# A hybrid attention and mixture-of-experts kernel on one core: 48 down projections in three rounded products, an opening cut into tiles, and the router's weights inside the actor's matrix

## The reference, cut to what matters

```python
probs = softmax(x @ router_w.T)                                # 8 experts
a_h = gelu(x @ actor_w1.T + actor_b1)                          # 50 hidden
sampled_k = argmax(clip(a_h @ actor_w2.T + actor_b2, -30, 30)) + 1
mask = rank(probs) < sampled_k                                 # keep the first k experts
scores = where(mask, probs, 0)
for e in range(8):
    g = x @ gate_w[e].T;  u = x @ up_w[e].T                    # 336 hidden each
    out += scores[:, e] * ((silu(g) * u) @ down_w[e].T)
```

## Time and profile before

| | us |
|---|---|
| median of 3 runs | 513.47 |
| lowest and highest | 507.74 and 513.87 |
| the profiled execution | 508.82 |
| its span, first to last instruction | 507.0 |
| mean granted TensorE clock | 0.997 |

### The profile page before, as it was taken

How to read it: one execution, slowest core, us unless ns; L and a number is a source line. 1 busy time by engine, 2 the same in 40 slices (tenths; PEclk the granted TensorE clock), 3 DMA queues, 4 the chain that set the end, 5 groups by cost and what they waited for, 6 DMA issues and landing times.

```text
span 507.0 us, 6599 instructions
## 1 busy us (share of the span) xinstructions
PE 490.1 (97%) x2152; PEld 350.5 (69%) x2152; DVE 297.5 (59%) x705; ACT 247.6 (49%) x435; POOL 294.6 (58%) x306
## 2 busy tenths in 40 slices
PE   7798899999999999999999999999999999999997
PEld 6576666677676666767677677776767676666666
DVE  3647343746767795497844889459673443723332
ACT  3286637356725674238552387425671345223221
POOL 4344778348759393493564737546455555665554
PEclk9999899999999999999999999999999999999999
DMA  8600000000000000000000000000000000000000
GB/s 241 228 0 2 0 0 2 0 1 1 1 1 1 0 0 2 1 2 0 1 0 2 0 1 1 0 2 21 1 0 1 1 22 0 0 1 21 0 2 21
DMA packets 7933, 7.38 MB, mean 15 GB/s; under 512 B 732, under 2 KB 7772, under 8 KB 7900
## 3 DMA queue, kind: packets, MB, share of 16 engines
q1 hardware_dynamic: 7900, 6.97, 4.5%
HBM read 5.91 MB, written 1.05 MB: 14 GB/s over the span
## 4 chain that ended last, share of the span: by engine, by line
PE 74%; DVE 6%; ACT 3%; issue 2%; POOL 1%; DVEq 0%; ACTq 0%; POOLq 0%
PE bank L1150 23%; PE bank L1000 14%; PE bank L1002 13%; PE bank L1001 13%; PE bank L1201 3%; PE bank L1104 1%; DVE t L929 1%; PE bank L1189 1%; PE bank L1020 1%; POOL t L566 1%; PE bank L1158 1%; ACT sl L678 1%; ACT xn L582 1%; PE bank L1138 1%; PE bank L1112 1%
## 5 line engine op out<-in xcount | busy, mean ns | idle before, releaser
L566 POOL TENSOR_TENSOR t<-t,sl 128x512 f32<-128x512 f32 x105 | 136.2, 1301 | 111.2 <-DVE t L929 86.8
L678 ACT ACTIVATE sl<-bank 128x512 f32<-128x512 f32 x168 | 98.9, 595 | 161.3 <-PE bank L1002 151.6
L1150 PE MATMUL bank<-t,WD 128*128 128x512 f32 x328 | 161.6, 592 | 0.0
L929 DVE TENSOR_TENSOR t<-bank,sbc 128x512 f32<-128x512 f32 x105 | 72.2, 688 | 89.9 <-PE bank L1002 88.8
L1000 PE MATMUL bank<-xhF,WGh 128*128 128x512 f32 x168 | 98.9, 589 | 3.4 <-ACT sl L678 2.7
L566 POOL TENSOR_TENSOR t<-t,sbc 128x512 f32<-128x512 f32 x63 | 81.4, 1318 | 8.9 <-ACT sbc L672 8.0
L1150 PEld LDWEIGHTS bank<-t,WD 128*128 128x128 f32 x328 | 61.7, 188 | 28.6 <-issue 15.1
L929 DVE TENSOR_TENSOR t<-bank,sl 128x512 f32<-128x512 f32 x63 | 42.9, 685 | 55.7 <-ACT sl L678 25.2
L1000 PE MATMUL bank<-xhF,WUh 128*128 128x512 f32 x168 | 67.4, 401 | 1.4 <-DVE t L929 1.4
L1002 PE MATMUL bank<-xhF,WUl 128*128 128x512 f32 x168 | 66.6, 397 | 0.0
L1001 PE MATMUL bank<-xlF,WUh 128*128 128x512 f32 x168 | 66.5, 396 | 0.0
(11 more groups left out here) (184 smaller groups left out, 669.7 us busy)
## 6 DMA issues: line engine op xcount, KB each, us to landing
stage<-in_gate SPq DMA_DIRECT2D x7, 192.0 KB, 5.7
stage<-in_up SPq DMA_DIRECT2D x7, 192.0 KB, 6.0
WD<-in_down SPq DMA_DIRECT2D x7, 192.0 KB, 6.0
X<-in_x SPq DMA_DIRECT2D x4, 256.0 KB, 5.7
out<-X SPq DMA_DIRECT2D x3, 256.0 KB, 2.3
raw<-in_small SPq DMA_DIRECT2D x1, 388.0 KB, 5.3
out<-X SPq DMA_DIRECT2D x2, 128.0 KB, 1.9
raw<-in_small SPq DMA_DIRECT2D x1, 192.0 KB, 2.7
```

The costliest lines, as they stand in the source:

```text
L566: pool.tensor_tensor(t2[k % NT2][:, :], t2[k % NT2][:, :], by[:, :], ALU.mult).then_inc(a_done, 1)
L678: act.activation(sl[k % NSL][:, :], bank[k % 2][:, :], ACT.Silu).then_inc(silu_done, 1)
L929: dve.tensor_tensor(t2[k % NT2][:, :], bank[2 + k % 2][:, :], by[:, :], ALU.mult).then_inc(t2_done, 1)
L1150: pe.matmul(OACC[:, :], WD[:, c, :], t2[k % NT2][:, :], start=(c == 0), stop=(c == CH - 1 or k == TAIL[0] - 1))\
```

## The change

It has three parts.

**Down projections.** For 48 of the 168 chunks, chosen by the planner from slot 29 on and none of TAIL, ACT rounds `t2` into a high part (`ah`, three buffers), DVE writes the low part over `t2` (step "al"), and PE adds three rounded passes in place of one fp32 product. `WD` is split once, in seven pieces, ACT the high and POOL the low part (step "wd", every second slot from slot 26). A chunk is taken when the planner's running loads for DVE, ACT and POOL are below three limits. A fp32 down product of another chunk keeps its form.

**Opening.** The head mask is built in two halves, the first ahead of the norm. The three norms that DVE does signal each tile, and PE begins with the first tile. The sums of squares are computed ahead of the similarity. The residual of batch 0 is added tile by tile from four banks. The transposes of the first F norm go to two banks and are split in halves, and the first two passes of gate 0 start before the low half of the tokens is there.

**Routing.** The router's eight columns sit at rows 64 to 71 of the actor's matrix, so that the actor's three passes give the logits too. ACT copies 72 rows in place of 50, and PE transposes the eight rows for four tiles (a new step "rt", one slot later), and DVE reads the logits from that bank. The exponential and its sum come one slot later in the list. The two bank turns of a routing step are now one for "route" and one for "rt".

Besides, `qF`/`kF` share their space with `ql`/`kl`, and `bt` with `PT`; a bank that "byx" frees counts as free one slot later, and the copies of the next transposed scores wait for it.

```diff
+SPLIT_FROM, WD_FROM = CH + 8, CH + 5
+NAH = 3
-F_STEPS = [(0, "stats"), (2, "xn"), (4, "xT"), (5, "xl"), (6, "route"), (7, "rexp"), (7, "inner", 0),
-           (10, "inner", 1), (9, "rsum"), (12, "rrank"), (12, "tanh"), (13, "gelu"), (15, "act"),
+F_STEPS = [(0, "stats"), (2, "xn"), (4, "xT"), (5, "xl"), (6, "route"), (7, "rt"), (7, "inner", 0), (8, "rexp"),
+           (10, "inner", 1), (10, "rsum"), (12, "rrank"), (12, "tanh"), (13, "gelu"), (15, "act"),
-            awo=(0, 0, .5), am=(.3, .3, 0), am2=(.3, .3, 0), y=(.9, 0, .6), route=(2, 1.1, .3), rexp=(0, 2.7, 0),
+            awo=(0, 0, .5), am=(.3, .3, 0), am2=(.3, .3, 0), y=(.9, 0, .6), route=(.7, 1.1, 0), rt=(.4, 0, .4), rexp=(0, 2.7, 0),
+COST |= dict(ah=(0, .6, 0), al=(0, 0, .9))
+DVE_LOAD = dict(uk=.7, al=.9, stats=1.4, xl=.7, ar=.6, ascale=.5, amax=.6, awo=.5, y=.7, yT=.7, rt=.8, rsum=3.6, rrank=2.9,
+                gelu=1.7, actk=1.6, bv=.7, bsp=1.2, byx=2.4)
+DVE_ROOM, DEBT_ACT, POOL_LEAD = 0.7, 1.0, 1.5
...
+    def halves(k):
+        room = debt[0] < DEBT_ACT and dve_load[0] < DVE_ROOM + DVE_LOAD["uk"] and pool_free[0] < k + POOL_LEAD
+        for j in split:
+            if ("al", j) not in done and slot_of.get(("ah", j), last) < k:
+                add(("al", j))
+                debt[1] += COST["al"][2]
+        j = seen[0]
+        while j < len(um_end) and um_end[j] < k + 0.5 and slot_of["um", j] < k:
+            weights = slot_of.get(("wd", j % CH // WCH), last) + 1 < k
+            if j >= SPLIT_FROM and j not in TAIL and weights and room:
+                split.append(j)
+                add(("ah", j))
+                debt[0] += COST["ah"][1]
+            seen[0] += 1
+            if j in split:
+                break
+            j += 1
...
-            if j < len(um_end) and um_end[j] + AFTER_POOL <= k and (j % CH or j == 0 or block_end[j // CH - 1] + OACC_REST < k):
+            if j in split:
+                due = slot_of.get(("al", j), last) < k
+            else:
+                due = j < seen[0] and um_end[j] + AFTER_POOL <= k
+            if due and (j % CH or j == 0 or block_end[j // CH - 1] + OACC_REST < k):
...
+        halves(k)
         products(k, 2)
+        if wds and k >= WD_FROM and k % 2:
+            add(wds.pop(0))
+            debt[0] += 0.5
...
@@ POOL @@
+            head_mask(range(H // 2))
                     if seq == 0:
-                        head_mask()
+                        head_mask(range(H // 2, H)).then_inc(consts_ready, 1)
+                if kind == "wd":
+                    pool.wait_ge(wdh_ready, s[1] + 1)
+                    pool.tensor_tensor(WDl[:, at, :], WD[:, at, :], WDh[:, at, :].bitcast(F32), ALU.subtract).then_inc(wdl_ready, 1)
@@ ACT @@
+                    if (what, b) == ("F", 0):
+                        act.wait_ge(half_full, 1)
+                        act.activation(xhF[0][:, 0:T // 2], bank[3][:, 0:T // 2], ACT.Copy).then_inc(xh_half, 1)
-                    act.activation(xa[:, :], m_bank(t + 1)[0:AH, :], ACT.Identity, bias=cols[0:AH, 4:5])
+                    act.activation(xa[:, :], m_bank(t)[0:R0 + E, :], ACT.Identity, bias=cols[0:R0 + E, 4:5])
+                if kind == "ah":
+                    k, i = s[1], split_at[s[1]]
+                    act.wait_ge(a_done, k + 1)
+                    if i >= NAH:
+                        act.wait_ge(down_done, split[i - NAH] + 1)
+                    act.activation(ah[i % NAH][:, :], t2[k % NT2][:, :], ACT.Copy).then_inc(ah_done, 1)
@@ DVE @@
+                    if s == ("y", 0):
+                        for i in range(NT):
+                            ...
+                            r = dve.tensor_tensor(X[:, i, :], bank[i][:, 0:P], X[:, i, :], ALU.add)
+                if kind == "al":
+                    k, i = s[1], split_at[s[1]]
+                    dve.wait_ge(ah_done, i + 1)
+                    dve.tensor_tensor(t2r[k % NT2][:, :], t2[k % NT2][:, :], ah[i % NAH][:, :].bitcast(F32),
+                                      ALU.subtract).then_inc(al_done, 1)
@@ PE @@
-                    for i in range(NT):
-                        a, o = slice(i * P, i * P + P), 3 * E * i
-                        pe.matmul(m[:, o:o + 2 * E], xh[:, a], router[:, :], start=True, stop=True)
-                        r = pe.matmul(m[:, o + 2 * E:o + 3 * E], xl[:, a], router[:, 0:E], start=True, stop=True)
-                    r.then_inc(m_full[t % 3], 1)
-                    m = turn(t + 1)
                     wh, wl = swide(C_ACTOR, P)
+                    three(m[:, :], wh, wl, xh[:, :], xl[:, :]).then_inc(m_full[t % 3], 1)
+                if kind == "rt":
+                    wait_free(pe, turn_of["route", n])
+                    for i in range(NT):
+                        r = pe.transpose(m[:, i * E:i * E + E], xa[R0:R0 + E, i * P:i * P + P], ident[R0:R0 + E, R0:R0 + E])
+                    r.then_inc(m_full[t % 3], 1)
+                    if k == 0:
+                        pe.wait_ge(xh_ready, split_no["F", 0] + 1)
+                        pe.matmul(bank[0][:, :], WGh[:, 0, :], xhF[0][:, :], start=True, stop=False)
+                        pe.matmul(bank[0][:, :], WGl[:, 0, :], xhF[0][:, :], start=False, stop=False)
+                    if k in split_at:
+                        pe.wait_ge(al_done, split_at[k] + 1)
...
+                    if k in split_at:
+                        i = split_at[k]
+                        r = three(OACC[:, :], WDh[:, c, :], WDl[:, c, :], ah[i % NAH][:, :], t2r[k % NT2][:, :],
+                                  start=(c == 0), stop=(c == CH - 1 or k == TAIL[0] - 1))
+                    else:
+                        r = pe.matmul(OACC[:, :], WD[:, c, :], t2[k % NT2][:, :], start=(c == 0), stop=(c == CH - 1 or k == TAIL[0] - 1))
```

More of the change, by code:

```diff
@@ L177, in plan, with bank_free @@
     um_end, downs, block_end = [], [0], []
+    split, seen = [], [0]
+    dve_load = [0.0]
+    slot_of = {}
+    wds = [("wd", j) for j in range(CH // WCH)]
+    def bank_free(by):
+        return by in done and (by[0] != "byx" or slot_of[by] < k)
     def ready(s):
@@ L192, in ready @@
         n = 0 if s[0] == "bo" and s[2] else TURNS.get(s[0], 0)
-        return all(len(free_after) + i < 3 or free_after[len(free_after) + i - 3] in done for i in range(n))
+        return all(len(free_after) + i < 3 or bank_free(free_after[len(free_after) + i - 3]) for i in range(n))
     def add(s):
@@ L197, in add @@
         done.add(s)
+        slot_of[s] = k
+        dve_load[0] += DVE_LOAD.get(s[0], 0)
         if s[0] in POOL_COST:
@@ L262, in plan @@
         debt = [max(0.0, act - pe), max(0.0, dve - pe)]
-    assert not any(th[1] for th in threads)
+        dve_load[0] = max(0.0, dve_load[0] - pe)
+    assert not any(th[1] for th in threads) and not wds
     while downs[0] < last:
@@ L281, in build @@
     xT_turn = {norm_no[s[1:]]: turn_of[s] for s in steps if s[0] == "xT"}
+    split = [s[1] for s in steps if s[0] == "ah"]
+    split_at = {k: i for i, k in enumerate(split)}
     split_no = {s[1:]: i for i, s in enumerate(s for s in steps if s[0] == "xT" and s[1] != "A")}
@@ L343, in build @@
         sx = sb("sx", [P, NT, E, P // E])
-        xa, hq = (sb(n, [AH, T]) for n in ("xa", "hq"))
+        xa, hq = sb("xa", [R0 + E, T]), sb("hq", [AH, T])
         YT = sb("YT", [P, T])
@@ L347, in build @@
         sl = [sb(f"sl{i}", [P, T]) for i in range(NSL)]
+        t2_at = cursor[0]
         t2 = [sb(f"t2{i}", [P, T]) for i in range(NT2)]
+        cursor[0] = t2_at
+        t2r = [sb(f"t2r{i}", [P, T], F32R) for i in range(NT2)]
+        WDh, WDl = (sb(n, [P, CH, P], F32R) for n in ("WDh", "WDl"))
+        ah = [sb(f"ah{i}", [P, T], F32R) for i in range(NAH)]
         xaT = [sb(f"xaT{i}", [P, T]) for i in range(2)]
@@ L406, in build @@
         tail_full, tail_added = sem("tail_full"), sem("tail_added")
+        wdh_ready, wdl_ready, ah_done, al_done = (sem(n) for n in ("wdh_ready", "wdl_ready", "ah_done", "al_done"))
         qf_ready, qkl_ready = sem("qf_ready"), sem("qkl_ready")
@@ L483, in chain, with head_mask @@
                 pool.wait_ge(pool_did, did[0])
-            def head_mask():
-                for e in range(H):
+            def head_mask(heads):
+                for e in heads:
                     own = hmask[:, e * DH:e * DH + DH]
@@ L598, in _ @@
                     dst = xhF[b % 2] if what == "F" else xhS
+                    if (what, b) == ("F", 0):
+                        a = slice(T // 2, T)
+                        act.activation(dst[:, a], m_bank(t)[:, a], ACT.Copy).then_inc(xh_ready, 1)
+                        continue
                     act.activation(dst[:, :], m_bank(t)[:, :], ACT.Copy).then_inc(xh_ready, 1)
@@ L752, in _ @@
                         dve.wait_ge(x_loaded[q], 16)
-                    else:
+                    elif (what, b) != ("F", 0):
                         wait_free(dve, turn_of[src])
@@ L1077, in _ @@
                         a = slice(i * P, i * P + P)
```

(11 more changed lines are left out.)

139 lines of the change are left out of this document (91 added, 48 removed).

## The result

The changed kernel takes 514.39 us in the median of 14 runs (512.71 to 517.22), the kernel before 510.14 us in its 14 (507.74 to 513.87). The ratio is 1.0083, 95% interval 1.0053 to 1.0113: slower, by 4 us, where 13 us less were forecast. The profiled execution has a span of 512.7 us, 5.7 us above that of before.

The account below looks back on a forecast made before the run. PE's own work was taken as the bound from about 50 us on. Down projections -7.8, routing -3.7, opening -2.5 and waits +1 made -13.0 us, from 513.47 to 500.5 us; forecast case 497.5 to 503, range 493.5 to 508.

Parts of the forecast that it names:

- Routing and opening: Router products replaced by four transposes, -3.7 us; first gate earlier through tile-wise norms, residual and split halves, -2.5 us.
- One sign: Expected in the profile after: no router products, four transposes of 0.44 us together, PE not idle ahead of them.
- The price of a split: Down projections: three rounded passes at 0.70 us for an fp32 product at 0.86, 0.163 us less each, -7.8 us for 48.
- DVE ahead of POOL: DVE's low-half subtraction goes before POOL's product, which is pushed back at most 0.69 us; chain fits with 0.7 to spare.
- The step that failed: WD pieces in slots 27 to 39 fit POOL's room for 7 us; waits in stretches with threads +1 us, bounds 0 and +6.
- The wait on "al": PE waiting for DVE's low half in stretches with threads, within +1 us; a POOL product ahead for five of 48: 6.5.
- the signs of being wrong: DVE or ACT releasing PE from 400 us on; "al" median near 1.3 us; opening's 3 us gone at 50 us.
- given back in part: Rival: saved PE time partly lost in stretches with threads as "al" meets POOL's products; +7 instead of +1, 506.5 us, chance 0.18.
- POOL first: Rival: the subtraction loses its place to POOL's product and PE waits for "al"; +26 us, 533 us, chance 0.07.

Follow-up runs that it names:

- e1: Changed kernel with no down product split and no WD pieces made, opening and routing alone: 501.81 us, 0.986 of the kernel before.
- e5: Like e2, with the planner still counting the WD pieces, but neither ACT nor POOL makes one: 513.67 us, 1.011 of the kernel before.
- e10: e2 with the statistics of B's third batch moved behind the products of chunks 69 and 70 in POOL's order: 506.81 us, 0.996 of the kernel before.
- e2: Changed kernel with the seven WD pieces made but no down product split: 513.51 us, 1.010 of the kernel before.
- e3: Changed kernel with WD pieces in slots 91 to 103 and splits only from chunk 118 on: 500.17 us, 0.983 of the kernel before.
- e14: Changed kernel, WD pieces uncounted in slots 91 to 103, 37 splits from chunk 119 without 127 and 135 to 137: 496.20 us, 0.975 of the kernel before.
- e7: e2 with all seven WD pieces made but not counted by the planner, other steps placed as in e1: 511.29 us, 1.008 of the kernel before.
- e13: Changed kernel, WD pieces uncounted in slots 3 to 9, 37 splits from chunk 118 without 127 and 135 to 137: 498.58 us, 0.982 of the kernel before.
- e11: e7 with a wait added on POOL behind the last WD piece, until DVE's rank operations and reciprocal are done: 503.83 us, 0.988 of the kernel before.
- e4: Changed kernel with WD pieces in slots 27 to 39 and splits only from chunk 118 on: 509.40 us, 1.001 of the kernel before.

## Why the prediction was wrong, step by step

**Routing and opening** held. Forecast -3.7 and -2.5, together -6.2; e1 has -7.0. One sign failed: in the changed kernel PE waits once, 1.9 us at 119 us, ahead of the new transposes; e1 hasn't that wait, while e5, with the order of the pieces, has it. In the changed kernel the first gate starts at 22.89 (forecast 22.6), and the four transposes start at 27.10, with the second gate pass at 27.78, so they take 27.78 - 27.10 - 0.23 = 0.45 us (forecast 0.44). PE, changed kernel:

```profile
22.89 0.53 PE L1243 MATMUL bank<-xhF,WGh 128*128 128x512 f32 x1
...
27.10 0.41 PE L1216 MATMUL bank<-ident,xa 8*128 8x8 f32 x4
...
27.78 0.40 PE L1106 MATMUL bank<-xlF,WGh 128*128 128x512 f32 x1
```

**The price of a split** held. Nine passes take 476.92 - 474.85 = 2.07 us in the changed kernel, where the earlier trace rows give 2.25: 0.18 less (forecast 0.163):

```profile
474.85 0.39 PE L1105 MATMUL bank<-ah,WDh 128*128 128x512 f32 x1
...
476.92 0.39 PE L1105 MATMUL bank<-ah,WDh 128*128 128x512 f32 x1
```

The page "TensorE: Matmul & The Clock Gate" of the Trainium skill (section "Wait — 56ns, not 53.3ns?") has 215.7 ns for a warm pass of 512 columns. Here too the trace has 0.23 us.

**DVE ahead of POOL** held for 44 of the 48. The low half takes 683 ns in the median; four took 1.05 to 1.77 us. POOL's product takes up to 1.75 us (1.80 in the form with `sbc`):

```profile
L1034 DVE TENSOR_TENSOR t2r<-t,ah x48: 675/683/1772, 147.3 to 502.5; 128x512 fp32r<-128x512 f32 x48
```

**The step that failed** is the one that gave the seven pieces nothing and all waits in the stretches with threads +1 us, bounds 0 and +6, on the ground that POOL, busy 35 of 50 us, "has room for 7 us". What came in its place is 19.7 us by the spans (5.7 more in place of the 14.0 less of the three gains), 18.2 by the medians. A share of the time was read as room, and from the wrong stretch. Slots 27 to 39 lie at 94 to 130 us in the kernel before, and not in the window from 50 to 100 us that the 35 us are from. The kernel before, at the end of these slots:

```profile
120.00:130.00 10.00, 9.63 (x38) 6.43 (x37) 7.10 (x11) 7.13 (x13) 9.84 (x9) 1.00 0.00 1
```

POOL is busy 9.84 of 10 us there. It works off a backlog of products: none can start before the first scores are there (slot 11), and from then on it gains on PE slot by slot. In the plan its product of chunk 63 stands 3 slots behind the gate in the kernel before and 5 in the changed one; from chunk 63 on, silu waits for POOL's product of two chunks earlier, so a backlog above one slot is PE's. I had read the switch between the two forms in the code and put no date on it. The largest wait came as neither of the prices I had given: a POOL step that waits for DVE, with urgent products behind it. That is 5.5 us with the clock's part (e10), of 11.8 for the pieces. The other stalls of e2, of 1.9 us at 119 and 2.5 us at 218 us, I didn't take away one by one, so their causes stay as the traces read. The wait on "al" was priced, but within that +1 us: with the clock's part it is a good part of what the early splits cost, as the trace reads.

Of the signs of being wrong one came true: from 400 us on, DVE and ACT appear as releasers of PE, for 1.2 and 1.1 us (e3's two waits). The other two didn't: the opening's gain is still there at 52 us, and "al" has its 683 ns.

Of the rivals, "given back in part" was right in kind and much too small: +7 in place of 18 to 20. "POOL first" had the right pair of engines but mostly the wrong place: "al" is held up four times, by 1.1 us at most, while DVE's routing operations can be starved.

## What to carry to other kernels

An engine at 60 or 70% can be on the path if it works off a backlog against a due time; ask when its queue must be empty, and count new work against that date. In a list that all engines follow in order, look at each wait for what stands behind it: moving one step of 0.2 us behind two products was worth 6 us. And a saved pass on the bounding engine was worth its full price (37 x 0.17 = 6.3 us in e14) where nothing else made PE wait, so put such an edit there and leave it out elsewhere.

## What the runs showed of the hardware

- A DVE operation with two SBUF inputs can wait not for one POOL operation but for a whole run of them: 7.53 us for 0.28 us of work in e7, through seven operations without a gap, 6.33 us in e13, and 1.38 us in e11, where POOL pauses. It doesn't always: in e7 another one took 1.51 us in the same run. The page "SBUF — State Buffer" of the Trainium skill (section "Who interferes with whom") calls the port pair that the two engines share an exclusive lock, for which a DVE instruction with two SBUF inputs contends with a GpSimd instruction that reads SBUF. The trace agrees on who excludes whom, but in e7 and e13 DVE didn't get its turn between back-to-back POOL instructions.
- A pause of PE can be paid twice. In e7 PE stands for 5.9 us, and of the work behind it 4.5 us are at 1.2 GHz; between chunks 41 and 43 e7 falls 7.9 us back against e1. A pause needn't be followed by it: that of 2.5 us near 218 us is in e4, with the clock at 1.2 GHz for 3.4 us, and not in e2.
